# Sums of the two plain passes go out eight units at a time, into a staging area

## The chip, the core and the metric

The kernel runs on one core of one Trainium2 chip. The metric is the device time of one execution in microseconds; the figure given for a kernel is the median of several executions. The profile is one further execution, taken with the hardware profiler.

## The reference

The reference is a stack of four graph layers on 6250 nodes with 256 channels, over 106,250 edges that are sorted by destination. Each layer normalizes the node rows, applies relu, and adds what the layer computes to the running rows x. L0 is a graph attention net of three layers in parallel, L1 is an attention layer combined with a selective scan in degree order and a feed-forward net. L2 and L3, which the change is about, are these:

```
L2: neighbor = segment_sum(edge_weight * h[src], dst)
    out = leaky_relu(h @ W1.T + b1 + (neighbor + neighbor * h) @ W2.T + b2, 0.2)
    x = x + out / max(norm(out), 1e-12)
L3: agg = segment_sum(h[src] , dst)          (then times M)
    x = x + relu(h @ W + agg @ M)
```

L3's kernel uses that the sum over edges and the product with M can be exchanged. All arithmetic is in float32.

## The kernel before

**Units and blocks.** The 6250 nodes are padded to 49 blocks of 128 (T = 49, NP = 6272). The sorted edge list is cut into units of 256 edges (UE) so that no unit serves two blocks; there are room for UNITS = 464 of them, and the last ones, past the real edges, are padding. A plan made on the chip early on (plan_units) orders the blocks by how many units they have, smallest first, and writes for each unit the source rows (unit_src), the position of each destination in its block (unit_rel), the weights (unit_w), whether the unit continues the block of the unit before (unit_keep), and, for a block's last unit only, the block's number (unit_block; all other units hold the value SKIP). Source numbers past the last edge come from the tail of a padded copy of src, which is filled with the one number NP: row NP of each table is a row of zeros.

**The two plain passes.** L2 and L3 each run one PlainPass (lines 1187 to 1340) over all 464 units. Unit u uses slot v = u mod 16 (RING) of a ring of source rows. These instructions belong to one unit:

- POOL issues two indirect DMAs, each of which gathers 128 rows of 1 KB (gather_all, L1222). Its only wait is for PE to have finished unit u - 16. POOL's instructions stand in one straight list of 928 gathers; the other engines run a loop.
- DVE makes two 128x128 one-hot matrices (one_hot, L1232 with weights, L1234 without).
- PE multiplies them with the gathered rows and adds both products in PSUM (sum_rows, L1243). It waits for the gathers, the one-hots and, because there are two PSUM buffers, for DVE's sum of the unit two before.
- DVE adds the product to the running sum (collect, L1252), two units behind. It writes one of eight buffers, so it waits for SP's store of the unit eight before.
- SP stores the sum (store_sums, L1257 to L1259), three units behind. It loads unit_block into a register, computes an address, and issues a DMA of 128 KB that is left out where the value is SKIP; its semaphore is advanced either way.

**Bundles.** A bundle is a DRAM table with three rows of 256 floats for each node: the sum, h and x. Gathers read the h rows (the index is 3 * src + 1). The sums are cleared in all blocks at the start of the kernel, by 98 DMAs on POOL's queue (clear_sums, L1396), for blocks without an edge.

**Posts.** Eight units are a half round. Beginning with the twelfth half round, each half round also does the dense work of one block whose sum is finished: L2's is interact (lines 2427 to 2441) and the layer norm that follows (renew), L3's is linear (lines 2457 to 2464). The instructions of a post are woven in between those of the units: the load of the block's bundle (384 KB, issued by ACT) stands after the first unit of the half round, and from the fifth unit on (the 4 in `steps = [(early(one, j), 4, 3)]`, L1293) three steps follow each unit. A post begins with transposes on PE (L2420), a copy out of PSUM by ACT (L2422), eight matmuls (o_f_ps, L2423), and then DVE (L2432 in L2, L2461 in L3). Before a post, ACT waits for the stores of the eight sum buffers (L1276 to L1278). Every engine runs its own list in order, so a DVE instruction of a post that waits holds back the one-hots and sums that stand behind it. The last posts of a pass come after its units, one after another.

The two passes of L0 and L1 (SegmentPass, gathers at L618 and L1000) use the same plan and the same src numbers, with rows of 768 and more floats.

Of the kernel before, what the change touches and what calls it, by code (L numbers as in the profile page):

```python
# [27 lines left out]
P = 128  # L28
# [156 lines left out]
def graph_stack_kernel(nc, a, out):  # L185
# [4 lines left out]
    with root:  # L190
# [24 lines left out]
        bundles = [scratch(f"bundle{k}", [(SKIP + 1) * P, 3 * D]) for k in range(2)]  # L215
# [48 lines left out]
        order_low = sb("order_low", [1, T], I32)  # L264
        start_i = sb("start_i", [P, NC], I32)
# [19 lines left out]
        with ExitStack() as local:  # L285
            lsb = maker(local, "sb")
            tail = EPAD - FRONT - E
            pad_i = lsb("pad_i", [1, tail], I32)
            pad_front = lsb("pad_front", [1, 2], I32)
            chain.apart((dve, lambda: dve.memset(pad_i[:, :], NP)),  # L290
# [13 lines left out]
            for b in bundles:  # L304
                copies.append(lambda b=b: sp.dma_start(b[NP:ROWS, :], zeros[:, 0:3 * D]))
# [881 lines left out]
        class PlainPass:  # L1187
# [5 lines left out]
            SUMS = 8  # L1193
# [3 lines left out]
            def __init__(self, stack, name, weighted, bundle, landed, seen):  # L1197
                lsb, lps = maker(stack, "sb"), maker(stack, "ps")
                self.weighted, self.bundle = weighted, bundle
                self.tab = at(bundle, 0, [[D, 3 * ROWS], [1, D]])  # L1200
                self.rows = lsb(f"rows_{name}", [P, RING, 2, D])
                self.hot = lsb(f"hot_{name}", [P, self.SUMS, 2, P])
# [3 lines left out]
                self.stored = [sem(f"stored_{name}{v}") for v in range(self.SUMS)]  # L1206
# [3 lines left out]
                for v in range(self.SUMS):  # L1210
                    sp.sem_inc(self.stored[v], 16)
# [14 lines left out]
            def one_hot(self, i, v):  # L1226
                u = i * RING + v
                dve.wait_ge(self.s_pe, u + RING - self.SUMS + 1)
                for e in range(2):
                    rel, w = unit_rel[:, ds(u, 1), e], unit_w[:, ds(u, 1), e]  # L1230
                    if self.weighted:
                        last = dve.tensor_scalar(self.hot[:, v % self.SUMS, e, :], iota[:, :], rel, w, ALU.is_equal, ALU.mult)  # L1232
                    else:
                        last = dve.tensor_scalar(self.hot[:, v % self.SUMS, e, :], iota[:, :], rel, None, ALU.is_equal)  # L1234
                last.then_inc(self.s_hot, 1)

            def sum_rows(self, i, v):
# [4 lines left out]
                for e in range(2):  # L1242
                    mm = pe.matmul(self.acc[:, v % 2, 0:D], self.hot[:, v % self.SUMS, e, :], self.rows[:, v, e, :],  # L1243
                                   start=(e == 0), stop=(e == 1))
# [45 lines left out]
            def run(self, early, late, one, two, per_one, per_two):  # L1290

                def posts(i, half, j, first=False):
                    steps = [(early(one, j), 4, 3)]  # L1293
# [32 lines left out]
                for v in range(self.SUMS):  # L1326
                    act.wait_ge(self.stored[v], 16 * (UNITS // self.SUMS + 1))
# [44 lines left out]
        with ExitStack() as local:  # L1372
# [18 lines left out]
            def clear_sums():  # L1391
                for t in range(T + 1):
                    yield pool.dma_start(summed[t * P:(t + 1) * P, :], zeros[:, :]).then_inc(emptied, 16)
                for b in bundles:
                    for t in range(T):
                        yield pool.dma_start(b[t * P:(t + 1) * P, 0:D], zeros[:, 0:D]).then_inc(emptied, 16)  # L1396

            def count_beside():
                clearing = clear_sums()
                for n in range(NodeCount.GROUPS):  # L1400
                    targets.one_hots(n, n % 2)
                    targets.products(n, n % 2)
                    for _ in range(2):
                        next(clearing, None)
# [31 lines left out]
        def plan_units(lsb, spare_sb, small, bank):  # L1436
# [21 lines left out]
            begins = lsb("begins", [P, 2])  # L1458
            place = lsb("place", [P, 1])
# [56 lines left out]
            for k, v in enumerate((units_t, delta)):  # L1516
# [13 lines left out]
                                                             ALU.mult, ALU.add))  # L1530
            yield chain.step(dve, lambda: dve.tensor_copy(cols[:, 0:1], lane[:, :]))
# [7 lines left out]
            yield chain.step(pe, lambda: pe.matmul(small[0:1, 256:256 + T], lane[0:T, 0:1], pair[0:T, 0, :], start=True, stop=True))  # L1539
            yield chain.step(pe, lambda: pe.matmul(row_ps[:, :], named[0:T, :], past[0:T, :], start=True, stop=True))  # L1540
            by_chunk = small[:, 128:128 + 2 * (UC // P)].rearrange("p (c k) -> p k c", k=2)
            total = upto_u[:, T - 1:T]
            yield chain.step(dve, lambda: dve.tensor_copy(order[:, :], small[0:1, 256:256 + T]))
            yield chain.step(dve, lambda: dve.tensor_scalar(order_low[:, :], small[0:1, 256:256 + T], float(T - 2), None, ALU.min))
# [82 lines left out]
        with ExitStack() as local:  # L1627
# [147 lines left out]
            pool.wait_ge(emptied, 16 * (3 * T + 1))  # L1775
# [519 lines left out]
        with ExitStack() as local:  # L2295
# [14 lines left out]
            chain.step(dve, lambda: dve.tensor_scalar(unit_src[:, :, :], unit_src[:, :, :], 3, 1, ALU.mult, ALU.add))  # L2310
# [8 lines left out]
            def merge(ch, k, b0, m):  # L2319
# [60 lines left out]
                yield ch.move(lambda e: e.dma_start(blk(bundles[0][:, 2 * D:3 * D]), a3))  # L2380
                yield from layer_norm(ch, a3, l3, st, relu=True)
                yield ch.move(lambda e: e.dma_start(blk(bundles[0][:, D:2 * D]), l3))
# [7 lines left out]
        with finish:  # L2390
# [26 lines left out]

            def multiply(ch, wa, wb):
# [76 lines left out]
```

## Time and profile before

| | us |
|---|---|
| median of three runs | 8496.55 |
| lowest and highest | 8486.33, 8499.98 |
| profiled execution | 8437.77 |
| its span, first to last instruction | 8436.0 |
| POOL busy / PE / DVE / ACT | 4451.5 / 5542.8 / 5075.4 / 3299.4 |

The page's 40 slices are 211 us each. The gathers of L2's pass begin at 5459.5 us and end near 6893; those of L3's go from about 6962 to 8374. Together these passes and what hangs on them are the last three eighths of the span. In them the DMA engines are 30 to 50% busy, PE about 55%, DVE 30 to 44%, POOL 60 to 64%: no engine is full.

How to read a view: in a table of windows, each row is a stretch, with its length, each engine's busy time and number of instructions, then the granted share of TensorE's clock, the busy share of the 16 DMA engines and what they moved. In a list of waits, each row says who stood idle for whom, the total in the stretch, how many times, and the longest. "remote" is a semaphore that was advanced by something that is not an instruction with a known end (a DMA, or a sequencer on behalf of one); "issue" is idle time for which nothing is recorded.

### The profile page before, as it was taken

The page shows a single profiled execution, that of the slowest core. Times are in us where ns is not written, and L with a number is a line of the kernel's source. Part 1 is how long each engine was busy: PE and PEld are TensorE (multiplying, and loading weights), DVE is VectorE, ACT ScalarE, POOL GpSimd, SP SyncE. Part 2 cuts the span into 40 slices and gives each one's busy share as a digit, 9 for nine tenths or more (in the row PEclk, how much of TensorE's full clock was granted, in tenths as well). Part 3 has the DMA queues.
Part 4 walks back from the last instruction along what each step waited for, and adds up shares of the span by engine and source line. Part 5 has one row for each costly group of instructions (what it writes and reads, how often), then busy time and mean ns, then how long its engine had stood idle before and what let it go on. Part 6 is the DMA issues. An engine that isn't in the chain of part 4 may idle for free. (4 is left out here: it accounts for less than half of the span.)

```text
span 8436.0 us, 108263 instructions
## 1 busy us (share of the span) xinstructions
PE 5542.8 (66%) x20087; PEld 3496.7 (41%) x20087; DVE 5075.4 (60%) x10802; ACT 3299.4 (39%) x11053; POOL 4451.5 (53%) x4404
## 2 busy tenths in 40 slices
PE   4757688888886466577777657645556654555555
PEld 4524344444443232344444445424434432334443
DVE  7769488888887535588888746434444442323332
ACT  1224566666664247688888744300000000000000
POOL 4230365566553530667777632266656646666664
PEclk9978899999998567799999889867777776677777
DMA  7132688888886633788888942233333353333335
GB/s 246 26 84 94 217 274 272 276 274 278 274 277 200 206 116 111 260 299 301 312 301 291 268 128 72 67 94 110 115 111 114 116 89 94 106 111 113 111 112 82
DMA packets 532219, 1477.04 MB, mean 175 GB/s; under 512 B 134848, under 2 KB 226252, under 8 KB 531211
## 3 DMA queue, kind: packets, MB, share of 16 engines
q0 software_dynamic: 239680, 842.82, 34.1%
q1 hardware_dynamic: 249532, 561.11, 18.9%
q10 hardware_dynamic: 42668, 69.51, 2.6%
q8 instruction: 102, 1.67, 0.1%
q14 instruction: 237, 1.93, 0.1%
HBM read 1196.53 MB, written 607.81 MB: 214 GB/s over the span
## 5 line engine op out<-in xcount | busy, mean ns | idle before, releaser
L1222 POOL DMA_INDIRECT rows_e<-bundle,unit_src x1856 | 1762.7, 950 | 1161.6 <-issue 491.5
L1243 PE MATMUL acc_e<-rows_e,hot_e 128*128 128x256 f32 x3712 | 1265.6, 491 | 1056.4 <-issue 534.4
L618 POOL DMA_INDIRECT rows_e<-table,unit_src x928 | 1027.6, 1107 | 879.6 <-PE acc_e L823 448.5
L1243 PEld LDWEIGHTS acc_e<-rows_e,hot_e 128*128 128x128 f32 x3712 | 837.0, 244 | 1453.0 <-issue 1104.6
L1000 POOL DMA_INDIRECT rows_e<-table,unit_src x928 | 1040.1, 1121 | 481.6 <-issue 251.7
L812 ACT ACTIVATE rows_e<-rows_e 128x64 f32<-128x64 f32 x4640 | 1118.9, 332 | 1.9
L1252 DVE SCALAR_TENSOR_TENSOR sums_e<-sums_e,unit_keep,acc_e 128x256 f32<-128x256 f32 x928 | 443.8, 478 | 1056.1 <-remote 556.6
L2422 ACT ACTIVATE turned_f<-turn_f 128x512 f32<-128x512 f32 x98 | 58.5, 597 | 2278.6 <-DMA given_f<-bundle 1132.7
L1084 ACT ACTIVATE rows_e<-rows_e 128x64 f32<-128x64 f32 x3712 | 925.0, 333 | 25.5 <-issue 20.5
L823 PE MATMUL acc_e<-rows_e,unit_w 128*128 128x512 f32 (+1 forms) x1856 | 714.3, 532 | 146.8 <-issue 112.8
L823 PE MATMUL acc_e<-rows_e,hot_e 128*128 128x512 f32 (+1 forms) x1856 | 639.0, 497 | 33.9 <-ACT rows_e L812 26.9
L823 PEld LDWEIGHTS acc_e<-rows_e,unit_w 128*128 128x128 f32 x1856 | 357.9, 202 | 431.1 <-issue 378.7
L805 DVE TENSOR_TENSOR rows_e<-rows_e 128x896 f32<-128x896 f32 x464 | 503.0, 1084 | 39.6 <-ACT rows_e L782 38.9
L823 PEld LDWEIGHTS acc_e<-rows_e,hot_e 128*128 128x128 f32 x1856 | 344.1, 190 | 328.7 <-issue 252.4
L847 DVE SCALAR_TENSOR_TENSOR sums_e<-sums_e,unit_keep,acc_e 128x780 f32<-128x780 f32 x406 | 413.9, 1019 | 103.0 <-PE acc_e L823 94.7
L2095 DVE TENSOR_TENSOR_SCAN hs<-decay,state,inp 128x896 f32<-128x896 f32 x224 | 464.3, 2073 | 10.8 <-ACT decay L2106 6.2
L2423 PE MATMUL o_f_ps<-w,turned_f 128*128 128x256 f32 x784 | 325.3, 588 | 208.2 <-ACT turned_f L2422 171.6
L2117 PE MATMUL y_ps<-prod_t,ident 128*128 128x448 f32 x900 | 433.9, 610 | 0.0
L1232 DVE TENSOR_SCALAR hot_e<-iota,unit_rel,unit_w 128x128 f32<-128x128 f32 x928 | 289.7, 354 | 112.3 <-issue 101.8
L2423 PEld LDWEIGHTS o_f_ps<-w,turned_f 128*128 128x128 f32 x784 | 234.5, 309 | 287.3 <-ACT turned_f L2422 193.0
L1700 PE MATMUL tab_ps<-wt,hn 128*128 128x512 f32 x588 | 308.3, 660 | 1.9 <-DVE score_at L1678 1.9
L491 POOL TENSOR_TENSOR stat<-stat,power 128x2 f32<-128x2 f32 (+1 forms) x150 | 125.4, 843 | 328.6 <-DVE stat L490 327.6
(457 smaller groups left out, 9249.7 us busy)
## 6 DMA issues: line engine op xcount, KB each, us to landing
bc<-bc_rows SPq DMA_DIRECT2D x228, 896.0 KB
summed<-sums_e SPq DMA_DIRECT2D x464, 390.0 KB
bundle<-sums_e SPq DMA_DIRECT2D x928, 128.0 KB
summed<-sums_e SPq DMA_DIRECT2D x464, 130.5 KB
given_f<-bundle ACTq DMA_DIRECT2D x98, 384.0 KB
rows_e<-table,unit_src POOLq DMA_INDIRECT x1856
hots<-hot_e SPq DMA_DIRECT2D x116, 256.0 KB
hots<-unit_w SPq DMA_DIRECT2D x116, 256.0 KB
```

The source lines that it names most:

```text
L618: pool.indirect_dma_start(self.rows[:, v, e, :], None, table, bass.IndirectOffsetOnAxis(unit_src[:, u, e:e + 1], 0)).then_inc(self.landed[ ...
L805: dve.tensor_tensor(r, r, by.unsqueeze(3).broadcast_to([P, 2, n, DH]), ALU.mult).then_inc(self.s_mul, 1)
L812: last = act.activation(r, r, ACT.Copy, scale=self.rows[:, v, e, self.WIDTH + h:self.WIDTH + h + 1])
L823: mm = pe.matmul(self.acc[:, v % 2, a0:a1], self.hot_of(v)[:, e, :], self.rows[:, v, e, a0:a1], start=(e == 0), stop=(e == 1))
L1000: pool.indirect_dma_start(self.rows[:, v, e, :], None, self.tab, bass.IndirectOffsetOnAxis(unit_src[:, u, e:e + 1], 0)).then_inc(self.land ...
L1084: last = act.activation(r, r, ACT.Copy, scale=self.rows[:, v, e, D + h:D + h + 1])
L1222: pool.indirect_dma_start(self.rows[:, v, e, :], None, self.tab, bass.IndirectOffsetOnAxis(unit_src[:, u, e:e + 1], 0)).then_inc(self.land ...
L1243: mm = pe.matmul(self.acc[:, v % 2, 0:D], self.hot[:, v % self.SUMS, e, :], self.rows[:, v, e, :], start=(e == 0), stop=(e == 1))
L1252: dve.scalar_tensor_tensor(self.sums[:, at_, :], self.sums[:, (v - 1) % self.SUMS, :], unit_keep[:, ds(u, 1)], self.acc[:, v % 2, 0:D], AL ...
L2095: dve.tensor_tensor_scan(hs[:, b, :], decay, inp[:, b, :], state[:, ds(STEPS * m + k, 1)], ALU.mult, ALU.add).then_inc(s_scan, 1)
L2117: mm = pe.matmul(y_ps[:, z, 0:HS], ident[:, :], prod[:, b, z * HS:(z + 1) * HS], start=False, stop=False, skip_group_check=True)
L2423: yield ch.step(pe, *[lambda c=c: pe.matmul(o_ps, turned[:, c, :], (wa, wb)[c // 2][:, c % 2, :], start=(c == 0), stop=(c == 3)) for c in ...
```

## The change

The bundles lose their third row: they hold only h and x, two rows for each node. The sums go to a new DRAM tensor `stage` that has, for each partition, one row of 256 floats for each unit, and a last row of zeros. Every eighth unit, SP stores the sums of eight units in one DMA of 1 MB, without a register load and without a condition. There are sixteen sum buffers instead of eight, in two halves; DVE waits for a store once for each half, at its first buffer. A post now loads h and x from the bundle (256 KB) and the sum from the stage (128 KB, at the row of the block's last unit, given by a new small table `ends`, or at the row of zeros for a block without units). A post's steps begin two units later (6 in place of 4). The 98 DMAs that cleared sums are gone. The tail of the padded src holds the numbers NP to NP + 127 in turn, so that the 128 rows of a padding gather are 128 different rows of zeros.

```diff
-        bundles = [scratch(f"bundle{k}", [(SKIP + 1) * P, 3 * D]) for k in range(2)]
+        bundles = [scratch(f"bundle{k}", [ROWS, 2 * D]) for k in range(2)]
+        stage = scratch("stage", [P, UNITS + 1, D])
...
+            chain.step(pool, lambda: pool.iota(pad_rows[:, :], [[0, -(-tail // P)], [1, P]], base=NP, channel_multiplier=0))
...
-            for pad in (src_pad, dst_pad):
-                copies.append(lambda pad=pad: sp.dma_start(row(pad[FRONT + E:EPAD]), pad_i[:, :]))
+            for pad, end in ((src_pad, pad_rows[:, 0:tail]), (dst_pad, pad_i[:, :])):
+                copies.append(lambda pad=pad, end=end: sp.dma_start(row(pad[FRONT + E:EPAD]), end))
...
-            SUMS = 8
+            SUMS, HOTS = RING, 8
...
             def collect(self, i, v):
                 u, at_ = i * RING + v, v % self.SUMS
                 dve.wait_ge(self.s_pe, u + RING + 1)
-                dve.wait_ge(self.stored[at_], 16 * (2 * i + v // self.SUMS + 1))
+                if v % UB == 0:
+                    dve.wait_ge(self.staged[v // UB], 16 * (i + 1))
...
             def store_sums(self, i, v):
-                u = i * RING + v
-                block = sp.value_load(unit_block[0:1, ds(u, 1)], min_val=0, max_val=SKIP)
+                if v % UB < UB - 1:
+                    return
+                u, half = i * RING + v, v // UB
                 sp.wait_ge(self.s_sum, u + 3)
-                sp.dma_start(self.bundle[:, 0:D][ds(block * P, P), :], self.sums[:, v % self.SUMS, :],
-                             cond=(block < SKIP)).then_inc(self.stored[v % self.SUMS], 16)
+                sp.dma_start(stage[:, ds(u - UB + 1, UB), :], self.sums[:, half * UB:(half + 1) * UB, :]).then_inc(self.staged[half], 16)
...
-                    for b in range(self.SUMS):
-                        act.wait_ge(self.stored[b], 16 * (2 * i + half))
+                    for h in range(2):
+                        act.wait_ge(self.staged[h], 16 * (i + max(half, 1 - h)))
                         act.sem_inc(act_passed, 1)
...
-                    steps = [(early(one, j), 4, 3)]
+                    steps = [(early(one, j), 6, 3)]
...
-                for b in bundles:
-                    for t in range(T):
-                        yield pool.dma_start(b[t * P:(t + 1) * P, 0:D], zeros[:, 0:D]).then_inc(emptied, 16)
...
+            yield chain.step(dve, lambda: dve.scalar_tensor_tensor(ends_f[:, :], begins[:, 1:2], -1.0, none[:, :], ALU.add, ALU.add))
...
+            def load_block(ch, j, bundle):
+                block, end = block_of(j), block_of(j, ends, UNITS)
+                return ch.move(lambda e: e.dma_start(given[:, 1:3, :].rearrange("p k d -> p (k d)"), bundle[ds(block * P, P), :]),
+                               lambda e: e.dma_start(s3, stage[:, ds(end, 1), :].rearrange("p o d -> p (o d)")))
...
             def interact(ch, j):
-                block = block_of(j)
-                yield ch.move(lambda e: e.dma_start(given[:, :, :].rearrange("p k d -> p (k d)"), bundles[0][ds(block * P, P), :]))
+                yield load_block(ch, j, bundles[0])
```

The plan gets five more small steps (three groups of arithmetic on DVE, one matmul and one copy) that make `ends`; linear loads by load_block as well, and the places that named the three rows of a bundle now name two.

## Rows read from the trace of the kernel before

**Rows 1.** The page's costliest group; columns as it explains them.

```profile
L1222 POOL DMA_INDIRECT rows_e<-bundle,unit_src x1856 | 1762.7, 950 | 1161.6 <-issue 491.5
```

**Rows 2.** Waits of POOL: all of L2's pass, then all of L3's.

```profile
POOL rows_e L1222 <- PE acc_e L1243: 195.0, 105, 4.3
...
POOL rows_e L1222 <- remote: 114.6, 56, 5.7
...
POOL rows_e L1222 <- PE acc_e L1243: 155.4, 66, 15.5
...
POOL rows_e L1222 <- remote: 129.3, 62, 6.5
```

**Rows 3.** Waits of POOL before the posts begin, 240 us of each pass.

```profile
POOL rows_e L1222 <- remote: 26.8, 10, 5.7
POOL rows_e L1222 <- PE acc_e L1243: 16.1, 14, 2.8
...
POOL rows_e L1222 <- remote: 24.7, 10, 6.5
POOL rows_e L1222 <- PE acc_e L1243: 14.0, 9, 3.0
```

**Rows 4.** Waits of DVE beside the posts, 1000 us of each pass.

```profile
DVE o_f L2432 <- PE o_f_ps L2423: 167.7, 29, 9.6
...
DVE sums_e L1252 <- remote: 95.3, 33, 5.8
...
DVE o_f L2432 <- issue: 36.8, 7, 6.1
...
DVE sums_e L1252 <- remote: 254.2, 57, 7.4
DVE given_f L2461 <- PE o_f_ps L2423: 238.1, 33, 13.8
```

**Rows 5.** SP's L1257: 6111 to 6122 us, then 6124 to 6127 (ns min/median/max).

```profile
L1257 SPq FUSED_REGOPS  x4: 691/705/710, 6110.9 to 6119.5; - x4
...
L1257 SPq SEQ_ASSERT  x2: 702/710/719, 6113.1 to 6120.2; - x2
...
L1257 SPq FUSED_REGOPS  x4: 42/103/164, 6124.1 to 6125.7; - x4
...
L1257 SPq SEQ_ASSERT  x2: 18/18/18, 6124.7 to 6125.9; - x2
```

**Rows 6.** Timeline, one post: PE's transposes and ACT's copy of them.

```profile
6113.36 0.60 PE L2420 MATMUL turn_f<-ident,given_f 128*128 128x128 f32 x4
...
6123.14 0.60 ACT L2422 ACTIVATE turned_f<-turn_f 128x512 f32<-128x512 f32 x1 [12.90 <-DMA given_f<-bundle]
```

**Rows 7.** Queue of the gathers: 73 us of real units, 73 us of padding.

```profile
q0 software_dynamic: 2231, 6.07, 29.8%
...
q0 software_dynamic: 2064, 5.67, 89.0%
```

**Rows 8.** Windows of L1's pass: real units, then padding (columns: all engines).

```profile
4700.00:4780.00 80.00, 62.27 (x214) 36.90 (x212) 74.90 (x114) 75.55 (x280) 63.55 (x55) 0.98 0.91 297
4780.00:4860.00 80.00, 41.49 (x128) 25.17 (x128) 47.81 (x74) 45.57 (x171) 36.10 (x34) 0.79 0.97 193
```

**Rows 9.** Windows of L3's gathers alone: beside the posts, then padding.

```profile
7250.00:8250.00 1000.00, 621.24 (x657) 0.73 0.38 112
...
8300.00:8374.00 74.00, 35.91 (x38) 0.68 0.83 87
```

**Rows 10.** Timeline, end of L2's pass: DVE waits for a post's load.

```profile
6905.26 0.42 DVE L2430 SCALAR_TENSOR_TENSOR given_f<-given_f 128x256 f32<-128x256 f32 x1 [8.48 <-DMA given_f<-bundle]
```

**Rows 11.** Windows of the first stage, all engines.

```profile
60.00:100.00 40.00, 16.34 (x186) 13.95 (x186) 37.25 (x69) 5.65 (x10) 26.14 (x48) 1.00 1.02 395
```

**Rows 12.** DMA issues; the last number is us to landing.

```profile
rg<-residual POOLq DMA_DIRECT2D x10, 768.0 KB, 7.5
```

**Rows 13.** ACT's register loads for the posts (ns min/median/max).

```profile
L2416 ACTq TENSOR_LOAD <-order x196: 5/288/1130, 5751.8 to 8426.5; - x196
```

More of the change, by code:

```diff
@@ L264, in graph_stack_kernel @@
         order_low = sb("order_low", [1, T], I32)
+        ends = sb("ends", [1, T], I32)
         start_i = sb("start_i", [P, NC], I32)
@@ L304, in graph_stack_kernel @@
             for b in bundles:
-                copies.append(lambda b=b: sp.dma_start(b[NP:ROWS, :], zeros[:, 0:3 * D]))
+                copies.append(lambda b=b: sp.dma_start(b[NP:ROWS, :], zeros[:, 0:2 * D]))
+            copies.append(lambda: sp.dma_start(stage[:, UNITS, :], zeros[:, 0:D]))
             for c in range(2):
@@ L1205, in __init__ @@
                 self.landed, self.seen = landed, seen
-                self.stored = [sem(f"stored_{name}{v}") for v in range(self.SUMS)]
+                self.staged = [sem(f"staged_{name}{h}") for h in range(2)]
                 self.s_hot, self.s_pe, self.s_sum = (sem(f"{n}_{name}") for n in ("hot", "pe", "sum"))
@@ L1209, in __init__ @@
                 dve.sem_inc(self.s_sum, 2)
-                for v in range(self.SUMS):
-                    sp.sem_inc(self.stored[v], 16)
+                for h in range(2):
+                    sp.sem_inc(self.staged[h], 16)
                 chain.step(dve, lambda: dve.memset(self.sums[:, self.SUMS - 1, :], 0.0))
@@ L1242, in sum_rows @@
                 for e in range(2):
-                    mm = pe.matmul(self.acc[:, v % 2, 0:D], self.hot[:, v % self.SUMS, e, :], self.rows[:, v, e, :],
+                    mm = pe.matmul(self.acc[:, v % 2, 0:D], self.hot[:, v % self.HOTS, e, :], self.rows[:, v, e, :],
                                    start=(e == 0), stop=(e == 1))
@@ L1275, in half_round @@
                 if steps:
-                    for b in range(self.SUMS):
-                        act.wait_ge(self.stored[b], 16 * (2 * i + half))
+                    for h in range(2):
+                        act.wait_ge(self.staged[h], 16 * (i + max(half, 1 - h)))
                         act.sem_inc(act_passed, 1)
@@ L1325, in run @@
                     self.store_sums(n - 1, v)
-                for v in range(self.SUMS):
-                    act.wait_ge(self.stored[v], 16 * (UNITS // self.SUMS + 1))
+                for h in range(2):
+                    act.wait_ge(self.staged[h], 16 * (self.ROUNDS + 1))
                 for j in range(2 * n - self.AFTER, T + 1):
@@ L1402, in count_beside @@
                     targets.products(n, n % 2)
-                    for _ in range(2):
-                        next(clearing, None)
+                    next(clearing, None)
                     yield
@@ L1539, in plan_units @@
             yield chain.step(pe, lambda: pe.matmul(small[0:1, 256:256 + T], lane[0:T, 0:1], pair[0:T, 0, :], start=True, stop=True))
+            yield chain.step(pe, lambda: pe.matmul(small[0:1, 320:320 + T], ends_f[0:T, 0:1], pair[0:T, 0, :], start=True, stop=True))
             yield chain.step(pe, lambda: pe.matmul(row_ps[:, :], named[0:T, :], past[0:T, :], start=True, stop=True))
@@ L1543, in plan_units @@
             yield chain.step(dve, lambda: dve.tensor_copy(order[:, :], small[0:1, 256:256 + T]))
+            yield chain.step(dve, lambda: dve.tensor_copy(ends[:, :], small[0:1, 320:320 + T]))
             yield chain.step(dve, lambda: dve.tensor_scalar(order_low[:, :], small[0:1, 256:256 + T], float(T - 2), None, ALU.min))
@@ L2452, in renew @@
                 block = block_of(j)
-                yield ch.move(lambda e: e.dma_start(bundles[1][:, D:3 * D][ds(block * P, P), :],
+                yield ch.move(lambda e: e.dma_start(bundles[1][ds(block * P, P), :],
                                                     renewed[:, :, :].rearrange("p k d -> p (k d)")))
             def linear(ch, j):
-                block = block_of(j)
-                yield ch.move(lambda e: e.dma_start(given[:, :, :].rearrange("p k d -> p (k d)"), bundles[1][ds(block * P, P), :]))
+                yield load_block(ch, j, bundles[1])
                 yield from multiply(ch, w3, w4)
```

25 lines of the change are left out of this document (15 added, 10 removed).

## The prediction, made before the change was run

> **What bounds the kernel now.** I read the page first for what the two plain passes spend, then the waits of POOL, DVE and ACT in them, then one post on the timeline, then windows over the ends of all four passes.
>
> No engine is full in the plain passes. The fastest they could go is POOL's issue of gathers: it takes 950 ns for one, and leaves 491.5 / 1856 = 0.26 us between two without waiting for anyone [rows 1], 1.21 us in all, so 928 x 1.21 = 1128 us for a pass. The passes' gathers take 1433 and 1412 us, and the difference is what POOL waits: 195.0 + 114.6 = 310 us in L2's pass and 155.4 + 129.3 = 285 us in L3's [rows 2]. POOL's one wait is for PE to be done with the unit 16 before, so this is time in which the ring was full and PE late. The whole gain that the passes can give is these 594 us.
>
> Why is PE late, if PE and DVE each need about half the time? The reader is to see three things.
> - SP's register instructions come in two speeds. Between 6124 and 6127 us one takes 18 to 100 ns, between 6111 and 6122 us about 700 ns [rows 5], and POOL was gathering all through that stretch. SP has about ten such instructions for each unit (load of unit_block, address, check, condition, conditional DMA), 7 us a unit at the low speed, while POOL delivers a unit in 2.4 us. SP falls behind, its store is what advances the semaphore, and DVE, with eight sum buffers, has to wait for it: that is "remote" before sums_e, 95 us per 1000 in L2 and 254 us per 1000 in L3 [rows 4].
> - A post stops DVE until PE has made o_f_ps: 167.7 + 36.8 = 204.5 us per 1000 in L2, 238 us in L3 [rows 4].
> - Part of this comes from ACT. PE's transposes were done at 6114.0 us, ACT copied them at 6123.1 [rows 6], when the slow stretch ended. So ACT suffers from the slow stretches too, with no instruction of SP in its way.
>
> **Part 1: SP's work per unit goes.** Removed are 928 register loads with their address work and conditional DMAs; 116 plain DMAs stay. The low speed may stay too, but three or four instructions per eight units are about 3 us of it, beside 19 us of POOL. So I let DVE's wait for SP vanish. How much of POOL's waiting goes with it?
> - Before the posts begin (280 us of each pass) SP is the one thing that holds DVE beyond its own work. POOL's waits there are 26.8 + 16.1 in 240 us of L2 and 24.7 + 14.0 in L3 [rows 3], scaled to 280 us 50 and 45, in sum 95. DVE's own sequencer is slow in the same stretches, so I take two thirds: 63 us.
> - Beside the posts, what is left of POOL's waits is 310 - 50 = 260 us in L2, and in L3 285 - 45 = 240, less 16 that belong to the padding (part 3), 224. I divide it as DVE's waits divide: SP's share is 95.3 / (95.3 + 204.5) = 0.32 in L2 and 254.2 / (254.2 + 238.1) = 0.52 in L3 [rows 4]. That gives 83 and 116 us.
>
> Sum: -262 us. Its ends are 0 (ACT and DVE's own slow steps fill what SP leaves) and -578 (POOL never waits). I stay near the middle, since the rows name two culprits of like size.
>
> **Part 2: the stores of 1 MB.** Now the last store of each block moves 128 KB, 49 in a pass, and the others move nothing; then 58 move 1 MB each, some 54 MB more a pass. At 395 GB/s, what the DMA engines move when full [rows 11], one is 2.65 us, 116 of them 307 us of DMA time. The engines are 38% busy beside the posts [rows 9], and a half round would have 2.65 us more in 20: 50 to 55%. The gathers run up to 16 units ahead, and what they lose in one burst they make up, so I take 0; the other end is 307 us, when nothing of it hides. Does the wait for the store come to bear? The nearest landing is 7.5 us for 768 KB [rows 12], so 10 us for 1 MB; a half is written again eight units after its store was issued, 19 us at POOL's pace. DVE waits only if it does eight units in under 10 us, and then the ring is refilled meanwhile: nothing. What stands behind DVE's wait is PE's next product, and behind that POOL.
>
> The Trainium skill ("DMA: Bandwidth & Descriptors", Rules for kernel authors) advises to join many small transfers into one of a megabyte or more. The same page (Issuing engines are not separate DMA queues) warns that all queues end on the same 16 engines and interleave, which speaks against this change, since it joins transfers that mostly moved nothing. Its measured 6.15 us for 1 MB would make 116 stores 713 us instead of 307; no store of that size is in this trace.
>
> **Part 3: padding names 128 rows.** In 73 us of L2's pass with real units the gathers moved 6.07 MB and held the DMA engines for 29.8% of the time; in the 73 us of its padding they moved 5.67 MB and held them for 89.0% [rows 7]. Reading one row 128 times costs three times the engine time. What does this cost the kernel?
> - L1: 55 gathers issued in 80 us of real units, 34 in the 80 us of padding, at a DMA share of 0.97 [rows 8]. At the old pace the 34 take 49 us: -31, and some 4 us for the backlog that drains after the last. -35.
> - L3: 657 gathers in 1000 us beside the posts, 38 in the last 74 us [rows 9]; at the old pace these take 58: -16.
> - L2: the rate of gathers is the same in both stretches, but the last post but two waits 8.48 us for a load queued behind them [rows 10]: -8.
> - L0: DVE and PE set its pace, I take 0.
>
> Sum: -59 us, between -25 (only the part in L1 that the windows show, with a little less speed) and -80.
>
> **Part 4: the rest.** The first stage loses 98 DMAs of 12.8 MB, at 395 GB/s 32 us of DMA time. But DVE is busy 37.25 of 40 us while they run [rows 11], so it gives little: -5, ends 0 and -30. The plan's five more steps stand between count steps of DVE: +5, ends 0 and 15; the two cancel. A post's load is one register load (0.29 us, [rows 13]) and one DMA more, 1.1 us with the instructions around them. Woven in they hide, since a post's first step now stands six units later. In the tail of each pass, where posts stand alone, they don't: two posts each, +4; and the last store is 1 MB, which ACT waits for, instead of four small ones in a row: +2 each. Together +8. Moving the steps from the fifth to the seventh unit gives PE and DVE two units (2 x 1.2 us) before they stop, and leaves the end of the post as much nearer to the next load; I take 0, between -2.4 x 94 / 2 and the same above nothing (+-113).
>
> **The sum.** -262 - 59 + 8 = -313 us. The profiled execution took 8437.8 us, 58.8 less than the median of the runs shown; taken off the median it is 8496.6 - 313 = 8184 us.
>
> **The rivals.**
> - A, POOL becomes the bound: with DVE free of SP, PE stays within 16 units and POOL never waits. For: in bursts a unit takes DVE and PE only 1.2 us. Against: ACT's late copy [rows 6], which has another cause. 594 - 16 = 578, + 59 - 8 = 629 less: 7868 us.
> - B, the slow steps are what counts and not whose they are: ACT's copy comes only when the gathers pause, and they pause only when the ring is full, so the ring has to fill once in each half round whatever SP does. For: rows 6. Against: L3's 254 us of "remote". Part 1 is nothing: 8497 - 59 + 8 = 8446 us.
> - C, on the other side: the stores' traffic isn't hidden. If the slow stretches come with DMA traffic, a burst at full rate makes them longer, and if the gathers land later by all of it, each half round grows by 2.65 us. It decides from the point at which this is more than what part 1 gives back, 262 / 116 = 2.3 us a half round. For: the slow stretches lie where gathers stream. Against: 60% of the DMA time is free. With part 1 at nothing, B's 8446 + 307 = 8753 us; with half of it, about 8600.
> - D, the change doesn't do what it says for padding, because 128 rows beside one another are as slow as one: 8184 + 59 = 8243 us, inside the range.
>
> **Chances.** Forecast with D 0.60, A 0.13, B 0.17, C 0.10. The likeliest one's own range is 8050 to 8320. For 8 in 10 I reach halfway into A and up to B: 7950 to 8450. A measurement of this kernel tells about 0.2% (17 us) from no change. Faster by more than that: 0.60 + 0.13 + 0.14 of B = 0.87; within it: 0.03 of B and 0.02 of C = 0.05; slower: 0.08.
>
> **What would show it.** Right: "remote" before sums_e gone or below 20 us per 1000; POOL's waits from 594 to about 330 us; half rounds of 22 to 23 us instead of 25; in L1's padding window as many gathers as before it, with the DMA share of the L2 padding near 30 to 40%. For A, POOL's waits under 50 us. For B, the "remote" gone and POOL's waits unchanged, with o_f_ps taking their place before DVE. For C, a DMA share over 0.6 in the passes and PE waiting for the gathers. The forecast is wrong if DVE comes to wait for the 1 MB stores, or if posts hold DVE longer than the 204 and 238 us they hold it now.

## The result and the profile after

The changed kernel takes 8581.19 us (median of four, 8556.58 to 8592.01) against 8492.06 us for the kernel before in the same measurement (8486.33 to 8499.98): ratio 1.0097, interval [1.0075, 1.0119]. The forecast was 8184 us, faster. It is slower by 1%, outside the range.

Which pass lost the time can be read from one row each. Windows over each pass's gathers alone, first before, then after (length, POOL busy, PE's granted clock, DMA share, GB/s):

```profile
5459.50:6893.30 1433.80, 883.28 (x927) 0.71 0.41 111
6961.50:8374.20 1412.70, 877.48 (x928) 0.71 0.40 107
```

```profile
5499.90:7059.70 1559.80, 879.08 (x928) 0.68 0.42 135
7130.10:8528.90 1398.80, 876.96 (x928) 0.70 0.46 145
```

L2's gathers take 126 us more and L3's 14 us less; POOL's own work is equal. L2 begins 40 us later, but that can't be put down to the change: e16 below, which is the kernel before up to this point, begins it at 5514.2 us, and e10, which is the changed kernel up to it, at 5449.0. What follows L2's and L3's gathers is within 3 us of before.

The page's group of the gathers and POOL's waits in L2's pass, then in L3's (who waited for whom: total, times, longest); they answer to [rows 1] and [rows 2]:

```profile
L1227 POOL DMA_INDIRECT rows_e<-bundle,unit_src x1856 | 1757.9, 947 | 1280.6 <-issue 497.4
...
POOL rows_e L1227 <- PE acc_e L1248: 281.3, 70, 9.0
...
POOL rows_e L1227 <- remote: 156.9, 63, 3.6
...
POOL rows_e L1227 <- remote: 142.2, 77, 5.5
POOL rows_e L1227 <- PE acc_e L1248: 124.6, 59, 6.8
```

POOL waits 438 us in L2, 128 more than before, with fewer and longer waits (the longest 9.0 us instead of 4.3), and 267 us in L3, 18 fewer. So the question is who holds PE in L2's pass. DVE's waits beside the posts, 1000 us of L2 and of L3, beside [rows 4]:

```profile
DVE o_f L2447 <- PE o_f_ps L2439: 350.0, 26, 15.9
DVE o_f L2447 <- DMA given_f<-stage: 112.1, 8, 16.0
DVE sums_e L1258 <- remote: 56.2, 20, 5.3
...
DVE o_f L2447 <- issue: 15.0, 1, 15.0
...
DVE sums_e L1258 <- remote: 301.7, 64, 7.4
DVE given_f L2475 <- PE o_f_ps L2439: 246.0, 36, 14.5
```

In L2 the post now stops DVE before o_f for 350 + 112 + 15 = 477 us per 1000. Before, it was 232: the prediction's 204.5 left out this line of the same stretch.

```profile
DVE o_f L2432 <- DMA given_f<-bundle: 27.1, 4, 6.8
```

In L3 little moved: the post 246 (238.1 before), and "remote" before the sums, which was to vanish with SP's work, 301.7 (254.2).

One post on the timeline of the changed kernel (start, duration, engine, line; in brackets the idle time before it and its releaser):

```profile
6224.47 0.60 PE L2436 MATMUL turn_f<-ident,given_f 128*128 128x128 f32 x4
...
6234.95 0.95 POOL L1227 DMA_INDIRECT rows_e<-bundle,unit_src  x1 [0.30 <-issue]
6237.92 0.60 ACT L2438 ACTIVATE turned_f<-turn_f 128x512 f32<-128x512 f32 x1 [17.80 <-DMA given_f<-stage]
...
6238.90 0.94 POOL L1227 DMA_INDIRECT rows_e<-bundle,unit_src  x1 [3.00 <-remote]
...
6242.39 0.42 DVE L2447 TENSOR_TENSOR o_f<-o_f_ps,b 128x256 f32<-128x256 f32 x1 [15.22 <-PE o_f_ps L2439]
```

PE's transposes are done at 6225.1. ACT, idle, copies them at 6237.9, 2 us after POOL's last gather of the burst ended at 6235.9. POOL had stopped because the ring was full. It is the picture of [rows 6], and it is rival B's. It holds for most posts and not for all: in 31 of the 45 posts beside L2's gathers the copy begins when POOL has stood still for over 1 us, in 14 it doesn't.

### The profile page after: what moved, and what is told of

Read it like the earlier page. It is cut to its first block and busy times, and to the rows that moved or that the text cites. A ratio compares the mean times of both kernels' runs of the same rounds, so it can differ in the third digit from the quotient of the medians.

```text
span 8590.2 us, 101264 instructions
## 1 busy us (share of the span) xinstructions
PE 5511.3 (64%) x20089; PEld 3496.1 (41%) x20089; DVE 5064.6 (59%) x10807; ACT 3303.3 (38%) x11053; POOL 4354.8 (51%) x4307
## 5 line engine op out<-in xcount | busy, mean ns | idle before, releaser
L1248 PE MATMUL acc_e<-rows_e,hot_e 128*128 128x256 f32 x3712 | 1184.8, 476 | 887.3 <-DVE sums_e L1258 416.1
L623 POOL DMA_INDIRECT rows_e<-table,unit_src x928 | 1025.8, 1105 | 888.3 <-PE acc_e L828 463.7
L1005 POOL DMA_INDIRECT rows_e<-table,unit_src x928 | 1016.7, 1096 | 521.2 <-issue 243.3
L2439 PE MATMUL o_f_ps<-w,turned_f 128*128 128x256 f32 x784 | 351.5, 626 | 572.0 <-DMA given_f<-stage 298.1
L810 DVE TENSOR_TENSOR rows_e<-rows_e 128x896 f32<-128x896 f32 x464 | 502.8, 1084 | 44.3 <-ACT rows_e L787 43.9
L2439 PEld LDWEIGHTS o_f_ps<-w,turned_f 128*128 128x128 f32 x784 | 238.1, 318 | 661.2 <-DMA given_f<-stage 315.7
L2105 DVE TENSOR_TENSOR_SCAN hs<-decay,state,inp 128x896 f32<-128x896 f32 x224 | 464.4, 2073 | 26.7 <-ACT decay L2116 13.5
L2447 DVE TENSOR_TENSOR o_f<-o_f_ps,b 128x256 f32<-128x256 f32 x49 | 20.8, 424 | 628.7 <-PE o_f_ps L2439 501.6
```

The costliest lines, as they stand in the source:

```text
L623: pool.indirect_dma_start(self.rows[:, v, e, :], None, table, bass.IndirectOffsetOnAxis(unit_src[:, u, e:e + 1], 0)).then_inc(self.landed[ ...
L810: dve.tensor_tensor(r, r, by.unsqueeze(3).broadcast_to([P, 2, n, DH]), ALU.mult).then_inc(self.s_mul, 1)
L1005: pool.indirect_dma_start(self.rows[:, v, e, :], None, self.tab, bass.IndirectOffsetOnAxis(unit_src[:, u, e:e + 1], 0)).then_inc(self.land ...
L2105: dve.tensor_tensor_scan(hs[:, b, :], decay, inp[:, b, :], state[:, ds(STEPS * m + k, 1)], ALU.mult, ALU.add).then_inc(s_scan, 1)
L2439: yield ch.step(pe, *[lambda c=c: pe.matmul(o_ps, turned[:, c, :], (wa, wb)[c // 2][:, c % 2, :], start=(c == 0), stop=(c == 3)) for c in ...
```

## The experiments

**Two kinds of chip.** The first three experiments ran on a chip where the kernel before took 7853.82 us, not 8492. The register steps of SP's store (L1257, ns min/median/max over both passes) tell the two apart; the kernel before on the first chip, then e2, which has the same code there, on the other:

```profile
L1257 SPq FUSED_REGOPS  x1784: 2/146/1412, 5463.1 to 8406.6; - x199
...
L1257 SPq SEQ_ASSERT  x928: 2/18/1397, 5463.6 to 8406.9; - x186
```

```profile
L1257 SPq FUSED_REGOPS  x1784: 42/164/177, 5362.3 to 7810.3; - x199
...
L1257 SPq SEQ_ASSERT  x928: 18/18/24, 5362.8 to 7810.6; - x186
```

In e2 neither kind takes over 177 ns. I call such a chip one without slow steps. Three chips of the study were such (before 7827 to 7854 us); in the other four measurements, the first among them, there were slow steps (8457 to 8510 us). Each ratio below is against the kernel before on the same chip. "L2" and "L3" are the times from the first to the last gather of a pass in the profiled execution.

| run | before on that chip | ratio and interval | L2 | L3 |
|---|---|---|---|---|
| **without slow steps** | | | | |
| e1_posts4 | 7853.82 | 0.9864 [0.9843, 0.9885] | 1166 | 1161 |
| e2_before_posts6 | 7853.82 | 1.0001 [0.9991, 1.0012] | 1166 | 1161 |
| e3_before_pad | 7853.82 | 0.9855 [0.9834, 0.9876] | 1166 | 1161 |
| e5_after_again | 7846.38 | 0.9882 [0.9858, 0.9906] | 1167 | 1161 |
| e6_posts4_again | 7846.38 | 0.9879 [0.9861, 0.9898] | 1166 | 1161 |
| e4b_small_store | 7846.38 | 0.9872 [0.984, 0.9905] | 1166 | 1161 |
| e7_dve_copy | 7846.38 | 0.9891 [0.987, 0.9912] | 1167 | 1163 |
| e13_before_posts6_again | 7826.78 | 0.9992 [0.9983, 1.0001] | 1165 | 1161 |
| e14_after_beside | 7826.78 | 0.9891 [0.9876, 0.9906] | 1169 | 1162 |
| e15_hybrid_beside | 7826.78 | 0.9879 [0.9864, 0.9894] | 1165 | 1161 |
| **with slow steps** | | | | |
| the change | 8492.06 | 1.0097 [1.0075, 1.0119] | 1560 | 1399 |
| e8_hold6 | 8456.99 | 1.0079 [1.0051, 1.0107] | 1516 | 1418 |
| e9_hold4 | 8456.99 | 0.9993 [0.9965, 1.0022] | 1426 | 1422 |
| e10_posts4_third | 8456.99 | 1.0063 [1.0039, 1.0088] | 1445 | 1501 |
| e12_pad_again | 8506.89 | 0.9974 [0.9963, 0.9986] | 1436 | 1410 |
| e11_hybrid | 8506.89 | 0.9965 [0.9949, 0.9982] | 1440 | 1407 |
| e4c_small_store | 8506.89 | 1.0113 [1.0074, 1.0152] | 1576 | 1393 |
| e7b_dve_copy | 8506.89 | 1.011 [1.0075, 1.0144] | 1545 | 1410 |
| e16_before_posts6_third | 8510.17 | 1.0133 [1.0111, 1.0155] | 1555 | 1408 |

The profiled kernel before has 1434 and 1413.

**e1 and e2: the place of the steps, one way in each kernel.** e1 is the change with `steps = [(early(one, j), 4, 3)]`, e2 the kernel before with the 6.

> The changed kernel with one thing undone: a post's steps begin after the fifth unit again, not after the seventh. Of the 154 us that the changed kernel's profile is longer, 126 lie in L2's pass beside the posts and none in L3's. Theory 'late steps': six steps of L2's post (L3's has none left over) now stand at the end of the half round with no unit between them, in the time in which the full ring waits for PE; expected is L2's pass back at 1434 us or a little less, and the whole at 8450 to 8480 us. Rival 'store traffic': the 1 MB stores are what costs, and L2's pass stays near 1560 us, the whole near 8580.

> The kernel before with the one edit that a post's steps begin after the seventh unit. 'Late steps': L2's pass grows by 100 to 140 us, L3's stays within 20, the whole 8590 to 8630 us. 'Store traffic': no change beyond 20 us, 8490.

e1 0.9864, e2 1.0001. In e2 both passes run at POOL's pace; POOL's waits in L2's pass:

```profile
POOL rows_e L1222 <- issue: 266.5, 875, 0.3
POOL rows_e L1222 <- PE acc_e L1243: 15.8, 52, 0.3
```

Without slow steps there is nothing to win or lose in the passes: 1166 and 1161 us are measured, for any place of the steps, with and without SP's work. My floor of 1128 was too low: it spread 491.5 us over 1856 gathers, but they were 1565 pauses of 0.3 us, so a gather takes 0.95 + 0.30 = 1.25 us and a pass 1160. The question of the steps stayed open until e16.

**e3: the padding alone**, the kernel before with

```diff
-            for pad in (src_pad, dst_pad):
-                copies.append(lambda pad=pad: sp.dma_start(row(pad[FRONT + E:EPAD]), pad_i[:, :]))
+            for pad, end in ((src_pad, pad_rows[:, 0:tail]), (dst_pad, pad_i[:, :])):
+                copies.append(lambda pad=pad, end=end: sp.dma_start(row(pad[FRONT + E:EPAD]), end))
```

> The kernel before with the one edit that source padding names 128 rows of zeros in turn. My prediction took 59 us for it (35 in L1, 16 in L3, 8 in L2): 8437 us. Rival: padding gathers are faster, but the ends of the passes are set by what stands behind them, and the whole gains less than 15 us, 8480 to 8490. In either case the DMA share over the padding of L2's pass should fall from 0.97 to about 0.4.

0.9855: 117 us, all that the change brings on such a chip (96 us in e5, 85 in e14), or more. L1's last 80 us, first in e2, then in e3 (PE, weight load, DVE, ACT, POOL busy, clock, DMA share, GB/s), beside [rows 8]:

```profile
4671.00:4751.00 80.00, 33.50 (x89) 20.27 (x90) 34.60 (x53) 30.87 (x115) 34.18 (x33) 0.68 0.97 167
```

```profile
4657.00:4737.00 80.00, 62.10 (x210) 37.94 (x211) 70.66 (x110) 69.47 (x259) 63.33 (x55) 0.94 0.86 307
```

33 gathers become 55. The queue of the gathers over the last 73 us of L2 (packets, MB, share of the engines' time), again e2 and e3, beside [rows 7]:

```profile
q0 software_dynamic: 2163, 5.93, 74.4%
```

```profile
q0 software_dynamic: 2808, 7.67, 37.0%
```

The backlog of slow gathers also stood behind each pass. Between L2's last gather and L3's first lie 71.6 us in e2 and 40.6 in e3, behind L3's last 84.7 and 36.3: 79 of the 111 us that lie between these two profiles. 31 more are in L1 (15 in its pass, 16 behind it).

**e5, e6, e4b, e7: repeated without slow steps.** The change itself, the change with the steps at 4, and the change with one suspect taken away each: the size of the stores (e4b and e4c leave the sums out of the result), and ACT's copy.

```diff
-                sp.dma_start(stage[:, ds(u - UB + 1, UB), :], self.sums[:, half * UB:(half + 1) * UB, :]).then_inc(self.staged[half], 16)
+                sp.dma_start(stage[:, ds(u, 1), :].rearrange("p o d -> p (o d)"), self.sums[:, v % self.SUMS, :]).then_inc(self.staged[half], 16)
...
-                               lambda e: e.dma_start(s3, stage[:, ds(end, 1), :].rearrange("p o d -> p (o d)")))
+                               lambda e: e.dma_start(s3, stage[:, UNITS:UNITS + 1, :].rearrange("p o d -> p (o d)")))
```

That is e4b and e4c; e7 and e7b have this:

```diff
-                yield ch.step(act, lambda: act.activation(turned[:, :, :], turn_ps[:, :, :], ACT.Copy))
+                yield ch.step(dve, lambda: dve.tensor_copy(turned[:, :, :], turn_ps[:, :, :]))
```

> The changed kernel itself, again. The first experiments ran on a chip on which the kernel before takes 7854 us and not 8492; in their traces no register instruction of SP in the passes takes the 700 ns that both first traces show in stretches, and POOL never waits for long in L2's and L3's pass (1166 and 1161 us, POOL's own pace). Theory 'two chips': where those slow stretches are absent, SP's work, the store's bytes and the late steps are all hidden, and the changed kernel is as fast as its variant with early steps, 7745 us (ratio 0.986). Where they are present, it is slower than before by about 1%. Rival: the change costs 1% on any chip, and moving the steps back is what gave 7746: then 7930 us.

> The changed kernel with a post's steps after the fifth unit again. With slow stretches: 'late steps' wants L2's pass at about 1434 us, 126 less than the changed kernel, L3's unchanged. Without them: equal to the changed kernel within 10 us.

> The changed kernel, but each staging store writes only the last of its eight units (128 KB in place of 1 MB), and the posts load the row of zeros: the sums are left out of the result. Same instructions and waits. 'Store traffic': with slow stretches L2's pass falls from 1560 to near 1434 us. 'Late steps': it stays within 25 us. On a chip without slow stretches both expect less than 15 us, because the passes run at POOL's pace.

> The changed kernel, but DVE and not ACT copies a post's transposes out of PSUM. In the first two traces ACT begins this copy up to 13 us after its input is there, about when POOL stops gathering. Theory 'ACT held': the hold is ACT's alone, DVE isn't held, and with slow stretches L2's pass loses the pause of each half round: 1560 to about 1300 us. Rival 'all held': DVE's instruction is held as long, L2's pass stays above 1500. Without slow stretches: no change within 10 us.

0.9872 to 0.9891, all with overlapping intervals. They show that the whole change is 1.2% faster on such a chip, and tell none of the suspects apart, since none shows a cost there.

**e8, e9, e10: chip with slow steps.** e10 is e1's kernel. e8 (steps at 6) and e9 (steps at 4) make POOL count its units on a semaphore `issued` and ACT wait, before the first steps of a post, until POOL has issued all that the ring takes:

```diff
+                    pool.sem_inc(self.issued, 1)
...
+                    if steps and w == steps[0][1]:
+                        act.wait_ge(self.issued, i * RING + half * UB + w + 16)
```

> The changed kernel with early steps once more, in case this chip shows the slow stretches (then L2's pass about 1434 us and the whole near 8450); on a chip without them 7745 us again.

> The changed kernel with what the first traces show put in by hand: POOL counts the units whose gathers it has issued, and before a post's first step on ACT (the copy out of PSUM) ACT waits until the gathers of the unit 15 ahead are issued, that is until the ring is full. 'Late steps': in each half round POOL then stands still from the full ring to the next unit that PE finishes, and L2's pass is 1500 to 1600 us, some 100 us or more over its twin with early steps; L3's pass is equal in both. Rival 'store traffic': both twins are equal within 25 us in L2 as well.

> The same with a post's steps after the fifth unit. 'Late steps': L2's pass about 1400 to 1450 us, near the 1434 of the first trace of before. Rival: equal to the twin with late steps.

e10's L2 is at 1445 us, 115 less than the change: the late steps are L2's loss. But e10's L3 is at 1501, 102 more, and as a whole e10 is still slower than the kernel before (1.0063). By the two ratios the late steps cost the changed kernel 0.3% as a whole, and not the 1.3% that e16 shows in the kernel before. DVE's waits in 1000 us of e10's L3, then POOL's in that whole pass:

```profile
DVE given_f L2475 <- PE o_f_ps L2439: 502.8, 37, 16.5
DVE sums_e L1258 <- remote: 152.5, 35, 6.2
...
POOL rows_e L1227 <- PE acc_e L1248: 289.4, 77, 8.2
```

So with early steps L3's stop is double (502.8 against 246.0 with late ones, 238.1 in the kernel before). What the changed kernel has there and the kernel before has not is its load, 384 KB in two DMAs where it was one, and its stores. The holds don't bring the passes below the kernel before: with steps at 4 both are near it (1426 and 1422), with steps at 6 L2 is 90 us longer than with 4. That twins with the same hold differ by this shows that the place of the steps counts by itself. But the moment at which ACT begins counts too: e9 differs from e10 by the hold alone, a wait more, and is 78 us faster (8452.3 against 8530.0), in L3 above all (1422 against 1501). Why, was not tried.

**e12, e11, e4c, e7b: a second chip with slow steps.** e12 is e3's kernel. e11 takes each pass's better place for the steps, `(early(one, j), 4 if late else 6, 3)`.

> The kernel before with padding rows in turn, on a chip that may have slow stretches. My working took 59 us; without slow stretches it brought 117. With them I now expect 60 to 110, so 8350 to 8400 us where before takes 8460 to 8490. Rival: where POOL's wait sets the pace, faster padding is hidden, under 20 us.

> The changed kernel with early steps in L2 and late ones in L3, the better of both as the two traces with slow stretches have them (L2 1445 us with early steps and 1560 with late ones, L3 1501 and 1399). With slow stretches: L2 1445, L3 1400, the whole 8425 to 8450 us, 0.3% below before. Without them 7745. Rival: the passes' times differ by chance, and the whole stays at 8530 or above.

> The changed kernel with 128 KB in place of 1 MB in each staging store, posts loading the row of zeros (the sums are left out of the result), now perhaps with slow stretches. 'Store traffic': L2 1434 us in place of 1560 and L3 down by as much. 'Late steps': both passes within 30 us of the changed kernel's 1560 and 1399.

> The changed kernel with DVE in ACT's place for the copy out of PSUM. 'ACT held': with slow stretches L2's pass falls from 1560 to about 1300 us, L3's from 1399 to about 1250. 'All held': above 1500 and 1380.

The padding is worth only 0.26% here. e11 at 0.9965 is the fastest measured with slow steps; its interval overlaps e12's. POOL's waits in L2's pass of e11, then of e4c:

```profile
POOL rows_e L1227 <- PE acc_e L1248: 174.6, 102, 5.5
POOL rows_e L1227 <- remote: 151.5, 68, 4.7
```

```profile
POOL rows_e L1227 <- PE acc_e L1248: 278.6, 55, 8.4
POOL rows_e L1227 <- remote: 172.0, 71, 4.6
```

e4c's stores move an eighth of the bytes, and L2 (1576) and L3 (1393) are no shorter: rival C is out. The bytes do take DMA time (shares of 0.42 and 0.46 in the change's two passes, 0.35 and 0.38 in e4c's), but it is hidden, and C's sign, a share over 0.6, isn't there. In e7b the copy is DVE's. DVE's waits in 1000 us of its L2:

```profile
DVE turned_f L2438 <- DMA given_f<-stage: 322.3, 36, 16.2
DVE o_f L2447 <- PE o_f_ps L2439: 157.3, 30, 5.6
DVE o_f L2447 <- DMA given_f<-stage: 54.4, 6, 11.2
```

The wait only moved: DVE stands idle up to 16.2 us before the copy, and begins it 7.5 us in the mean, at most 13.5, after PE's transposes have ended. ACT does so 10.0 us after them in the change, 9.6 in e16, 5.6 in e11 and 3.3 in the kernel before; without slow steps it is 0.04 us on either engine (e2, e14, e7). The hold isn't ACT's own.

**e13 to e16: the late steps alone.** e13 and e16 are e2's kernel, e14 the change, e15 e11's kernel.

> The kernel before with nothing changed but the steps at the seventh unit. If the left-over steps alone cost L2 its time, a chip whose before takes about 8490 us shows L2's pass at 1545 to 1565 us instead of 1434, L3's near 1413, ratio 1.010 to 1.015. If it takes the new load too, L2 stays under 1460 and the ratio within 0.3% of 1. On a chip whose before takes 7850 us: 1.000.

> The whole change on the same chip. Left-over steps: 1.008 to 1.012, no slower than the steps alone on an 8490 us chip, since the padding gives some back. On a 7850 us chip 0.988.

> The change with L2's steps at the fifth unit and L3's at the seventh. 0.9965 on an 8490 us chip; 0.988, as the whole change, on a 7850 us chip, where the steps' place does not count.

> As e13: the steps alone. 1.010 to 1.015 and L2 at 1545 to 1565 us on an 8490 us chip if the left-over steps are enough by themselves; within 0.3% of 1 if they need the new load; 1.000 on a 7830 us chip, which would leave it open.

e13 fell on a chip without slow steps and gave 0.9992 [0.9983, 1.0001], as e2. e16 had slow steps: 1.0133 with one number changed in the kernel before. POOL's waits in its L2 pass, and DVE's in 1000 us of it:

```profile
POOL rows_e L1222 <- PE acc_e L1243: 282.7, 71, 7.8
...
POOL rows_e L1222 <- remote: 146.2, 70, 5.0
...
DVE o_f L2432 <- PE o_f_ps L2423: 267.9, 26, 15.0
...
DVE o_f L2432 <- issue: 100.0, 10, 11.7
```

It is the changed kernel's picture, 429 us of waiting for POOL (438) in few and long waits, in the code of before. The new load, the staging area and the stores aren't needed for it.

What the late steps do can be read behind the stop. The end of one, in the kernel before and in e16:

```profile
6127.60 0.42 DVE L2432 TENSOR_TENSOR o_f<-o_f_ps,b 128x256 f32<-128x256 f32 x1 [8.22 <-PE o_f_ps L2423]
6128.06 0.42 DVE L2433 SCALAR_TENSOR_TENSOR o_f<-o_f 128x256 f32<-128x256 f32 x1
6128.41 0.60 DVE L1232 TENSOR_SCALAR hot_e<-iota,unit_rel,unit_w 128x128 f32<-128x128 f32 x2
```

```profile
6231.92 0.42 DVE L2432 TENSOR_TENSOR o_f<-o_f_ps,b 128x256 f32<-128x256 f32 x1 [11.72 <-issue]
...
6233.93 0.48 DVE L2440 SCALAR_TENSOR_TENSOR renewed_f<-o_f,norm_f,given_f 128x256 f32<-128x256 f32 x1
6234.62 0.60 DVE L1232 TENSOR_SCALAR hot_e<-iota,unit_rel,unit_w 128x128 f32<-128x128 f32 x2 [0.20 <-issue]
```

From o_f to the next unit's one-hots DVE needs 0.80 us in the mean of L2's posts with steps at 4 (the kernel before, e10, e11), and 2.55 us with steps at 6 (the change, e16, e4c, and e2 too, where POOL isn't waiting).

## Why the prediction was wrong

Two steps failed. The larger is part 1, SP's work, at -262 us: the runs show about 0. The other turned what was left into a loss, the late steps in part 4 at 0: the runs show +108.

**The late steps.** The words are "Moving the steps from the fifth to the seventh unit ... I take 0, between ... (+-113)". Where steps are slow it is +108 us for the whole kernel before (e16), near the far end of that range. L2's pass alone takes 1555 us in e16, 1560 in the change and 1576 in e4c, against 1440 to 1445 with the steps at the fifth unit in the changed kernel and 1434 in the kernel before. 0 is right on the chips without slow steps alone (e2, e13). It lies in L2 and not in L3. L2's post has 12 steps, the load among them: from the fifth unit on, three after each of the last four units, none is left over. From the seventh, five are left (the expectation of e1 says six) and run after the half round's last unit with no unit between. L3's post has 6 steps and fits either way. The rows at the end of the last section show what the leftovers cost directly: 2.55 - 0.80 = 1.75 us in each half round before PE gets its next unit. Over the 47 posts beside the units that is 82 us, if all of it falls into POOL's pause, of the 119 that POOL waits longer in e16 (429 against 310). What makes the other third is open. The copy comes later after the transposes as well (9.6 us against 3.3), and a half round with more steps per unit, which would leave none over, was not run.

**Part 1, SP's work (-262), was nothing.** The cleanest place is ahead of the posts. DVE's waits in 240 us there, before, then after:

```profile
DVE sums_e L1252 <- remote: 73.3, 13, 10.2
...
DVE sums_e L1252 <- DMA bundle<-sums_e: 26.6, 6, 6.5
```

```profile
DVE sums_e L1258 <- remote: 111.0, 25, 10.2
```

The 26.6 us in which SP's store was late are gone, and "remote" took their place: 99.9 before, 111.0 after. The first 88 units take 252.6 and 251.8 us, on the chips without slow steps 221. The whole passes say the same: e12 has SP's work and e11 has not, on one chip, and L2 and L3 together take 2846 and 2847 us (8482.8 and 8473.8 us for the whole, intervals overlapping).

I took "remote" for SP's semaphore. In the changed kernel DVE waits for a store only at one sum in eight, but in the 1000 us of L3 63 of the 64 "remote" waits, 298.5 of 301.7 us, stand before other sums. It isn't PE either: its product for that sum had ended at least 2.6 us before DVE began, 7.4 in the median. One of them, with the products that ended before it:

```profile
7814.81 4.85 PE L1248 MATMUL acc_e<-rows_e,hot_e 128*128 128x256 f32 x20 [0.31 <-DVE sums_e L1258]
...
7825.72 0.48 DVE L1258 SCALAR_TENSOR_TENSOR sums_e<-sums_e,unit_keep,acc_e 128x256 f32<-128x256 f32 x1 [5.50 <-remote]
```

What is left is DVE's own sequencer. That is shown by exclusion only, since the profile has no slow instruction of DVE in this gap. This was rival B, to which I gave 0.17. Of its signs, POOL's waits are unchanged in L3 (267 for 285 us) and not in L2, o_f_ps took the place of "remote" before DVE in L2 alone, and "remote" gone failed, as it did for the forecast. The forecast's own sign of being wrong came true in L2, where posts hold DVE longer. B's 8446 us took the late steps at 0 as well: with +115 it would be 8561.

**Part 2, the stores, held**: 0 (e4b, e4c). No wait of DVE is put down to one, and the first 88 units are as long with the small stores of e4c (252.6 us). The seven eighths of the bytes that e4c leaves out took some 220 us of the DMA engines' time (the shares above times the lengths of the passes), where the prediction's 2.65 us a store make 269, and none of the kernel's time. The Trainium skill ("DMA: Bandwidth & Descriptors", Rules for kernel authors) advises to join small transfers into large ones. Here the joined stores of e11 can't be told from the single ones of e12 by the time, with the DMA engines under half busy in both (0.46 and 0.37 in L2).

**Part 3, padding, held in its mechanism**, the faster gathers, and its size depends on the chip: -59 was said, -24 measured in e12 and -117 in e3. L1's last 80 us in the changed kernel, where [rows 8] has 34 gathers, and the queue in the last of L2 (25.0% for 89.0%):

```profile
4811.00:4891.00 80.00, 56.10 (x184) 34.13 (x183) 60.96 (x94) 62.21 (x227) 59.78 (x54) 0.89 0.79 279
```

```profile
q0 software_dynamic: 2058, 5.63, 25.0%
```

What I missed is the time behind each pass (79 us in e3); that a full ring of slow gathers drains there before the last posts can go, is argued. Rival D (one beside the other as slow as one row) is out. With slow steps the two stretches behind the passes shrink by only some 10 us from the kernel before to e12, and the 35 us said for L1 don't show: its pass takes 1460 us before, 1475 after and 1479 in e12. Why padding is worth less there stays open.

**The rest of part 4**: the tails, +8 said, are within 3 us by the profiles. The first stage and the plan, said to cancel, cost about 11 us: L0's gathers begin at 928 to 932 us in the six profiles with the old plan and at 934 to 947 in the fourteen with the new one. Left out was that the changed kernel's L3 takes 102 us more where posts begin early (e10); the late steps, which cost L2 its time, save L3 from it. Whether it is the second DMA, the wait for the staging area or the stores that costs it, was not tried apart.

**The sum from runs**: late steps +108 (e16), padding -24 (e12), first stage and plan +11, SP's work 0: +95 us; +89 was measured. The terms come from several chips, so an agreement this close is partly luck.

## What to carry to other kernels

Shifting where a woven-in block of work begins is no free edit: count how many of its steps still find a unit to stand beside, and try it alone before it goes in with three others. An idle "remote" wait names no culprit; before it is priced as another engine's lateness, look whether it also stands where that engine isn't waited for. A gather's padding is better spread over many rows than put on one: look for its price behind the pass, not only in it.

## What the runs showed of the hardware

- The same kernel takes 7827 to 7854 us on three chips and 8457 to 8510 us in the other four measurements, 8% more. In the latter SP's register instructions (L1257) take some 700 ns, up to 1412, in stretches in which POOL streams gathers, where e2 has 177 at most; and ACT or DVE begins a post's copy up to 13.5 us after its input is there, where it is 0.04 without slow steps. L2's and L3's passes take 1166 and 1161 us without them and 1434 and 1413 with them. PE's granted clock in them is 0.71 with, 0.81 and 0.83 without (e2); whether it falls because PE waits more wasn't tried apart. What makes the steps slow stays open.
- A kernel can be 1.2% faster on one kind of chip (0.9882, 0.9891) and 1% slower on the other (1.0097). Of the versions run on both, two were faster on both: e11's, 0.9965 and 0.9879, and the padding alone, 0.9974 and 0.9855.
- Gathers that read one row 128 times against gathers of 128 rows, over 73 us: 74.4% and 37.0% of the DMA engines' time, the latter for 29% more bytes.
